# Token pooling and attention merged into one pipeline, with a new output product, on one Trainium2 core

## The reference

```python
def tok(x, w, b):                        # windows of 8 times: 750 -> 94 tokens
    xp = pad(x).reshape(B, F, 94, 8).transpose(0, 2, 3, 1)
    weights = softmax(einsum('bwkf,of->bwko', xp, w) + b, axis=2)
    return sum(xp * weights, axis=2)     # 128 x 94 x 64
def attn(x, Q, K, VO):                   # 8 heads, rank 32
    q = einsum('btd,hrd->bhtr', x, Q); k = einsum('bud,hrd->bhur', x, K)
    a = softmax(einsum('bhtr,bhur->bhtu', q, k) / sqrt(64), axis=-1)
    return einsum('bhtd,hde->bte', einsum('bhtu,bud->bhtd', a, x), VO)
h = tok(x, w, b)
h = h + attn(layernorm(h), Q, K, VO)
h = h + ffn(layernorm(h), ...)           # 4 heads x 4 experts, the same in both kernels
```

## Time and profile before

| | |
|---|---|
| median of 3 runs | 1125.67 us (1123.84 to 1126.86) |
| the profiled execution's own time | 1129.79 us |
| its span | 1128.0 us |
| TensorE busy | 985.3 us (87%) |
| VectorE busy | 931.5 us (83%) |
| ScalarE busy | 674.2 us (60%) |
| GpSimd busy | 676.0 us (60%) |

### The profile page before, as it was taken

One profiled execution on the slowest core, in us unless ns is written; L12 is line 12 of the kernel. 1 busy time (PEld: TensorE's weight loads), 2 busy tenths in 40 slices (PEclk: granted clock), 3 DMA queues, 4 the chain that ended last, 5 costly groups with the idle time before them and its releaser, 6 DMA issues.

```text
span 1128.0 us, 40703 instructions
## 1 busy us (share of the span) xinstructions
PE 985.3 (87%) x16376; PEld 681.6 (60%) x16376; DVE 931.5 (83%) x2061; ACT 674.2 (60%) x1719; POOL 676.0 (60%) x991
## 2 busy tenths in 40 slices
PE   5889878898898988986899999999999999999952
PEld 4667644454454544544677677777777776777741
DVE  3565539999999999982799999999999999999852
ACT  0111137777777777761666767767767667667621
POOL 2000036666656666541048788788888887788786
PEclk9999869999999999996899999999999999999975
DMA  7664300000000000000000001000000000010000
GB/s 256 192 207 125 113 1 2 2 2 2 1 0 0 0 0 0 2 1 6 15 10 15 16 15 23 18 16 20 14 15 19 11 20 18 12 22 19 20 8 14
DMA packets 41576, 35.31 MB, mean 31 GB/s; under 512 B 28160, under 2 KB 31232, under 8 KB 41472
## 3 DMA queue, kind: packets, MB, share of 16 engines
q1 hardware_dynamic: 41376, 33.83, 10.9%
q0 software_dynamic: 96, 0.00, 0.0%
HBM read 24.95 MB, written 3.08 MB: 25 GB/s over the span
## 4 chain that ended last, share of the span: by engine, by line
PE 48%; DVE 25%; POOL 12%; issue 8%; ACT 4%; DMA 1%; DVEq 1%; POOLq 0%; SPq 0%; ACTq 0%
PE psum L733 8%; DVE mx L1569 5%; PE psum L716 4%; PE psum L608 4%; PE psum L623 3%; DVE yc L1611 3%; PE psum L870 3%; PE psum L708 3%; PE psum L881 3%; PE psum L885 3%; PE psum L726 3%; POOL pu L459 3%; DVE xn L1561 2%; PE psum L855 2%; PE psum L889 2%
## 5 line engine op out<-in xcount | busy, mean ns | idle before, releaser
L459 POOL TENSOR_TENSOR pu<-pu,pr 128x752 f32<-128x752 f32 x96 | 138.7, 1444 | 127.7 <-DVE pr L1490 127.7
L524 POOL TENSOR_TENSOR st<-st,neg_half 128x12 f32<-128x12 f32 x64 | 145.8, 2278 | 5.0
L1189 ACT ACTIVATE pu<-psum,mx 128x94 f32<-128x94 f32 x512 | 124.6, 358 | 15.7 <-DVE mx L1481 14.5
L1272 ACT ACTIVATE pT<-psum 96x512 f32<-96x512 f32 (+1 forms) x224 | 126.4, 594 | 6.2 <-PE psum L870 3.3
L1569 DVE TENSOR_REDUCE mx<-psum 128x16 f32<-128x1536 f32 (+2 forms) x96 | 116.6, 1215 | 15.7 <-PE psum L855 11.5
L870 PE MATMUL psum<-ident_w,pu 128*96 128x128 f32 (+1 forms) x896 | 119.9, 275 | 1.9 <-ACT pT L1272 1.5
L1572 DVE TENSOR_TENSOR pu<-psum,mx 128x1536 f32<-128x1536 f32 (+2 forms) x96 | 117.6, 1225 | 3.3
L1266 ACT ACTIVATE pu<-pu 128x1536 f32<-128x1536 f32 (+2 forms) x96 | 101.8, 1060 | 10.0 <-DVE pu L1572 8.2
L733 PEld LDWEIGHTS psum<-vo_w,cT 128*128 128x128 f32 x768 | 90.7, 196 | 24.4 <-issue 13.0
L870 PEld LDWEIGHTS psum<-ident_w,pu 128*96 128x96 f32 (+1 forms) x896 | 100.8, 135 | 6.9 <-ACT pT L1272 4.3
L1422 DVE TENSOR_TENSOR xt<-psum,tok_pT 128x512 f32<-128x512 f32 x96 | 61.4, 684 | 50.5 <-PE psum L608 50.2
(11 more groups left out here) (178 smaller groups left out, 2324.8 us busy)
## 6 DMA issues: line engine op xcount, KB each, us to landing
xs<-in_x SPq DMA_DIRECT2D x64, 375.0 KB, 4.4
vb<-va SPq DMA_DIRECT2D x32, 128.0 KB, 2.3
out_h<-ho SPq DMA_DIRECT2D x128, 16.0 KB, 1.4
out_h<-ho SPq DMA_DIRECT2D x128, 7.5 KB, 1.4
vc<-va SPq DMA_DIRECT2D x96, 16.0 KB, 1.8
gx<-in_L_ffn_gate_w SPq DMA_DIRECT2D x16, 0.2 KB
fc<-in_L_ffn_fc_w SPq DMA_DIRECT2D x12, 1.0 KB
fc<-in_L_ffn_fc_b SPq DMA_DIRECT2D x12, 0.1 KB
```

Source lines behind the costliest of these rows:

```text
L459: pool.tensor_tensor(p, p, bcast(pr[:, j, :, :].rearrange("p a b -> p (a b)"), 2, NTOK), ALU.mult).then_inc(at_normed, 1)
L524: pool.tensor_tensor(st[:, k, 3, :], st[:, k, 2, :], neg_half[:, 0:NJ * NH], ALU.pow).then_inc(rstd, 1)
L1189: ins = act.activation(pu[:, j, par, hp, 0:NTOK], psum[:, (low, high)[par], NTOK * hp:NTOK * hp + NTOK], ACT.Exp, bias=mx[:, j, par, hp:hp ...
L1272: act.activation(pT3[j][:, f - (0, 4, 6)[i], :, :, :].rearrange("p e b t -> p (e b t)"), psum[0:rows, bank, :], ACT.Copy).then_inc(p_copie ...
```

## The change

1. The token and attention stages become one pipeline. Each engine has one function `quad(q)` with four steps, unrolled 48 times in all (no loop). Step `g` works on quad `g + 11` for token scores, on `g + 7` for the token softmax, on `g + 4` to `g + 6` for turning, scaling and pooling, and on `g + 2` down to `g - 3` for attention. Token scores and turned weights share bank 0; all else has banks 1 to 7, each with several users, and the waits for free banks are written out. The order of the calls on each engine was found by a search.
2. `exp_s` asks ScalarE for the sum of each exponential (`accum_out`) into `pl`; VectorE's reduction stays for part 1 only.
3. `give_out` becomes two products: `give_outT` with `vo_w` stationary (128 x 64) and 192 columns of `cT` moving, in two halves of the output columns; `copy_oT` on ScalarE; and a turn back by 64 x 64 products with the identity.
4. `make_g`, `make_w` and `make_w2` move into the pipeline. Groups of `x` are loaded one or two ahead of use as before, but the small loads of the experts' weights stand between groups 2, 3 and 4.

The core of the diff (waits left out where "..." stands):

```diff
                         ins = act.activation(pu[:, j, par, hp, 0:NTOK], psum[:, (low, high)[par], NTOK * hp:NTOK * hp + NTOK], ACT.Exp,
-                                             bias=mx[:, j, par, hp:hp + 1], scale=-1.0)
+                                             bias=mx[:, j, par, hp:hp + 1], scale=-1.0, accum_out=pl[:, j, par, hp:hp + 1])
...
-                dve.tensor_reduce(pl[:, j, :, :], pu[:, j, :, :, 0:NTOK], AX.X, ALU.add).then_inc(done, 1)
-                dve.wait_ge(done, 2 * g + 1)
+                if j in (1,):
+                    dve.tensor_reduce(pl[:, j, :, :], pu[:, j, :, :, 0:NTOK], AX.X, ALU.add).then_inc(done, 1)
+                    dve.wait_ge(done, 2 * g + 1)
                 dve.reciprocal(pr[:, j, :, :], pl[:, j, :, :]).then_inc(done, 1)
...
+            def give_outT(bank):
+                for hp in range(HP):
+                    for half in range(2):
+                        mm = pe.matmul(psum[64 * half:64 * half + 64, bank, 0:NT * 64].rearrange("p (j c) -> p j c", j=NT), vo_w[:, hp, :],
+                                       cT[:, hp, :, 2 * half:2 * half + 2, :].rearrange("p j b t -> p j (b t)"),
+                                       start=(hp == 0), stop=(hp == HP - 1))
+                mm.then_inc(at_outT, 1)
             def give_out(bank):
                 for j in range(NT):
-                    for hp in range(HP):
-                        mm = pe.matmul(psum[:, bank, NFEAT * j:NFEAT * j + NFEAT], cT[:, hp, j, :, :].rearrange("p b t -> p (b t)"), vo_w[:, hp, :],
-                                       start=(hp == 0), stop=(hp == HP - 1))
+                    for half in range(2):
+                        rows = slice(64 * half, 64 * half + 64)
+                        mm = pe.matmul(psum[rows, bank, NFEAT * j:NFEAT * j + NFEAT], oT[rows, j, :, :].rearrange("p b t -> p (b t)"),
+                                       ident[rows, 64 * half:64 * half + 64], start=True, stop=True)
...
+            def copy_oT(bank):
+                act.activation(oT[:, :, :, :].rearrange("p j b t -> p (j b t)"), psum[:, bank, 0:NT * 64], ACT.Copy).then_inc(at_oT, 1)
```

More of the change, by code:

```diff
@@ L341, in _ @@
             for n in range(NH):
-                load(2 + n)
+                if n == 0:
+                    load(2)
                 for e in range(NE):
@@ L368, in _ @@
                 slow(bet[:, 1, HD * i:HD * i + HD], fnorm_b.partition_broadcast(128))
+            for G in range(4, NGROUP):
+                load(G)
             def move_v(p):
@@ L609, in turn @@
                                       xs[:, GP * (G % 2) + 2 * Q + pair, 128 * c:128 * c + 128], ident)
[L610 to L627, removed]
@@ L643, in tok_turn, with make_g @@
                 pe.transpose(tok_P(), tok_e[:, :, :].rearrange("p w k -> p (w k)"), ident[0:TP, 0:TP]).then_inc(tok_turned, 1)
+            def make_g():
+                pe.wait_ge(attn_loaded, 16 * 4)
+                for half in range(2):
+                    for i in range(2):
+                        for par in range(2):
+                            hd = 2 * (2 * i + half) + par
+                            mm = pe.matmul(psum[64 * half:64 * half + 64, 0, 64 * (2 * i + par):64 * (2 * i + par) + 64],
+                                           k_w[:, hd, :], q_w[:, hd, :], start=True, stop=True)
+                mm.then_inc(g_made, 1)
@@ L806, in _ @@
-            for q in range(7, 9):
-                attention(q)
+                        elif exists(g, NQUAD):
+                            pe.wait_ge(at_xT, g + 1)
+                        elif exists(g + 3, NQUAD):
+                            pe.wait_ge(x_scaled, 3 * g + 11)
+                        elif exists(g - 3, NQUAD):
+                            pe.wait_ge(at_cT, 4 * g - 10)
+                        turn(g + 6, 2, 4)
+                    if exists(g + 11, NQUAD):
+                        if exists(g + 7, NQUAD):
+                            pe.wait_ge(tok_ready, ((g + 7) // 4) + 1)
+                        if exists(g + 7, NQUAD):
+                            pe.wait_ge(g_ready, 1)
+                        tok_score(g + 11)
@@ L809, in _ @@
+            for q in range(-3, 9):
+                quad(q)
             pe.wait_ge(causal_set, 10)
@@ new lines, in quad @@
+                    if exists(g, NQUAD):
+                        dve.wait_ge(at_scored, 3 * g + 3)
+                        least(g, 1, 5, 6)
+                        sums(g, 0)
+                    if exists(g + 5, NQUAD):
+                        dve.wait_ge(x_filled, 3 * g + 16)
+                        scale_x(g + 5, 2, 4)
+                    if exists(g, NQUAD):
+                        dve.wait_ge(at_exped, 3 * g + 2)
+                        sums(g, 2)
+                    if exists(g + 7, NQUAD) and (g + 7) % 4 == 0:
+                        dve.wait_ge(tok_scored, g + 11)
+                        soft_tok(g + 7)
@@ L1534, in attention @@
[L1534 to L1545 removed]
+                        dve.wait_ge(at_scored, 3 * g + 4)
@@ L1548, in stats3 @@
+                        least(g + 1, 0, 5, 6)
+            for q in range(-3, 9):
+                quad(q)
+            dve.wait_ge(at_added, NQUAD)
             def stats3(g):
```

676 lines of the change are left out of this document (373 added, 303 removed).

## The result

The changed kernel takes 1054.44 us, against 1124.97 us for the kernel before, run in turn on the same chip: a ratio of 0.937 [0.936, 0.939], 70.5 us saved. Forecast were 1056 us and 69.4 us.

A forecast was written before the change was run, and what follows sets the result against it. VectorE was taken to bound the old attention stage, TensorE the merged pipeline at 12.2 us a quad. Stages summed to 1058.6 against 1128.0 us, 69.4 us saved, so 1056 us from the median 1125.7; range 1028 to 1094.

The forecast's parts named there:

- the part that stays: TensorE's work in the old attention quad without `give_out`: 9.52 - 2.82 = 6.70 us a quad.
- The argument that I gave for it: Old `give_out` pairs follow at 0.12 us, less than their load (2.75/24 = 0.115 us) and a stream.
- The returned sums don't bind: ScalarE: 0.1 us per sum, 9.9 us a quad, below TensorE; rival at 0.3 us each: 1083 us, chance 0.12.
- The rings stand just behind: Merged quad: longest ring of waits found 11.4 us, under TensorE's 11.9 but near, so 2% added: 12.2 us.
- The one that I traced, through `turn_p`: Ring from VectorE's `least` for part 2 over transpose, `project`, `mix` and TensorE's `score` back to `least`: 11.4 us.
- the rival in which it falls: Merged stretch: granted clock falls; at 0.75 the quad takes 15.9 us, 100 us more, 1156 us; chance 0.05.
- first `mix`: End of part one: start, four quads of tokens alone, then 28 us of filling; at 64 us, 8 either way.
- The period: Steady merged quads 12.2 us apart (TensorE's 11.9 us plus 2%); 27 quads, 329.4 us.
- The weight products: `make_w` and `make_w2` moved between quads: 4.5 us once, on TensorE at the full clock.
- The drain: The last two attention quads, taken to drain as in the kernel before: 19.9 us.
- The saving is the token stage laid under attention: The prediction's reason for the 69.4 us saved, paid back by 1.5 us on each of 27 quads.
- VectorE works 10.36 us and bounds the stage: Old attention stage: VectorE's period is 10.74 us a quad with 0.38 us idle, so it was taken as the bound.

The follow-up runs named there:

- e7: The changed kernel with half of `give_outT` left out (two of four head pairs): 1046.44 us, 0.930 of the kernel before.
- e12: The changed kernel in its own order, with the experts' first normalisation done during the drain and the token softmax's bias addition removed: 1040.51 us, 0.923 of the kernel before.
- e3: The changed kernel with parts 2 and 3 both undone, the order of instructions kept: 1121.4 us, 0.995 of the kernel before.
- e1: The changed kernel with part 2 undone, all three `pl` reductions back on VectorE: 1084.74 us, 0.963 of the kernel before.
- e2: The changed kernel with part 3 undone, the old `give_out` back and its addition one quad earlier: 1088.87 us, 0.967 of the kernel before.
- e4: The kernel before with part 2 alone: 1128.49 us, 1.002 of the kernel before.
- e5: The kernel before with part 2, and GpSimd's wait for `mix` before writing `xn` made one quad later: 1130.75 us, 1.007 of the kernel before.
- e6: The kernel before with only GpSimd's wait for `mix` before writing `xn` made one quad later, without part 2: 1125.59 us, 1.0015 of the kernel before.
- e8: The changed kernel with `norm_tok`, the token weights' turn and `copy_tok` moved to other places in every fourth quad: 1064.64 us, 0.944 of the kernel before.
- e10: e8 plus the experts' first normalisation done early, and `pu` part 1 double-buffered, its transpose behind the next quad's `least` for part 1: 1075.39 us, 0.954 of the kernel before.

## Why the prediction was right, step by step

The bound and its size were right: TensorE, at 11.89 us a quad. That the total came within 2 us is in part luck. The span was 1052.4 us where the sum gave 1058.6 us, 6 us less, and its terms were off by up to 5.7 us in both directions. The forecast of the time hides this, as it was counted down from an execution of 1129.79 us, which lay 4.8 us above the median of 1124.97 us.

**TensorE is the bound, at 11.9 us a quad.** Measured 11.89 us. The terms moved against each other: the part that stays took 6.45, not 6.7 us (the two calls of `project` now follow each other, 1.56 instead of 1.70 us); the token work 3.53, not 3.1 us (`tok_score` 1.01, `pool_x` 0.79, three turns 1.69, and a quarter of the 0.17 us of the weights' turn); `give_outT` 1.45, where 1.4 was taken between 0.8 and 1.7; the turn back 0.50, where 0.7 was taken between 0.4 and 1.4. The 0.03 us by which the sum was off are errors of -0.25, +0.43, +0.05 and -0.20 us that cancel. As said, weight loads hide behind running products although both column halves use all 128 rows: a pair takes 1.45/16 = 0.09 us, and one of its loads alone has a record of 0.137 us. The argument that I gave for it does not hold, as 2.75/24 = 0.115 us is the distance from one load to the next and not a load's length; the record of one load of the old product is 0.192 us, at 0.12 us a pair. This is what the Trainium skill ("TensorE: Matmul & The Clock Gate", Part 2) allows with its background weight buffer, and not what its Part 3 would give.

**The returned sums don't bind.** 0.09 us each, 16 x 0.09 = 1.4 us a quad, where 0.1 us was taken between 0 and 0.18. By the Trainium skill ("ScalarE: Activation LUTs", What ACT_TABLE_LOAD costs) one more ACTIVATE of hardly any columns would cost its 186 ns of fixed time less 93 ns of overlap, so 93 ns as an estimate; the page gives no price for the accumulator, but the number fits.

**The rings stand just behind.** 11.4 us was predicted, and 2% laid on top for it. In ordinary quads nothing had to be laid on top. e7 shows a ring of 11.54 us. In the quads without token scores, where TensorE has less to do, a second one of 11.74 us shows, from `least` for part 1 back to itself through the second `project`, `mix` and everything up to the `score` for part 1; TensorE waits 0.65 us for VectorE in it. The one that I traced, through `turn_p`, was not the longest of the three; as no run makes it the bound, its 11.4 us stand untested.

**The clock holds.** 0.99 in the merged stretch; the rival in which it falls did not come.

**The sum by stages,** predicted and measured: first `mix` 64 and 67.5 us; to the 28th `mix` 333.9 and 329.2 us; three quads without tokens 31 and 31.4 us; drain 19.9 and 14.2 us; experts 609.7 and 610.2 us. Errors of +3.5, -4.7, +0.4, -5.7 and +0.5 us make -6 us of span. The terms that were mis-sized:
- *The period.* Ordinary quads 11.89 us, the mean over all but the weight products' excess 11.94 us, against 12.2 us: 7 us less. Every fourth is 12.66 us; the sum had spread the token softmax over four quads, and no term foresaw that it would delay one of them.
- *The weight products.* 6.65 us, against 4.5 us. The products themselves stand on TensorE's timeline for 1.33 + 3.67 = 5.0 us, 0.38 us of it idle. The rest is what follows: from 175.9 to 179.8 us the granted clock is 0.60 and 0.54, near the lower of the two levels, although TensorE had been busy all the time with products of 16 rows, and a `score` takes 1.44 instead of 0.79 us. e12, with another instant of the same work, kept 1.00 there and needed 16.54 - 11.89 = 4.65 us.
- *The drain.* It was taken as before; it fell to 14.2 us, at a granted clock of 0.88 (the window from 428.0 to 442.2 us) instead of 0.74. How much of the 5.7 us is the clock wasn't measured.

**What was wrong is the reason given for the gain.** "The saving is the token stage laid under attention" treats the merge as the gain and the other two parts as small corrections. e3 shows that the merge alone, in this order, gives 0.5%: attention's quad rises from 10.74 to 13.71 us, every fourth to 15.2, a mean of 14.1, where the two stages one after the other pay 10.74 + 3.85 = 14.59 us. The 70 us come from the three together. In the merge alone VectorE's work stands at 12.25 us, TensorE's at 12.78 us and a ring at 13.71 us, and each of the other parts lowers two of the three; with both in, the quad falls to 11.89 us. Undoing part 2, 1.8 us more of VectorE, costs 0.73 us a quad and 30 us in all (e1). Undoing part 3, 0.9 us more of TensorE and the addition moved, costs 1.09 us a quad and 34 us (e2), and both together cost 67 us (e3).

Before the merge the returned sums pay nothing (e4). The step that failed there is my reading of the earlier trace rows, "VectorE works 10.36 us and bounds the stage". The 10.36 us are right, but rings of 10.7 to 10.8 us held the stage (the chains of the kernel before, e4, e5 and e6), and VectorE's idle 0.38 us in each quad agrees with that. The forecast didn't suffer, as its sum for the merged pipeline was made anew from each engine's work. Part 3 alone on the kernel before wasn't tried.

## What to carry to other kernels

Sum the work of each engine and also the rings of waits, and look for how many of them are equal: an engine that is freed pays only as far as the next of them, which can be nothing (e4) or 0.73 of 1.8 us (e1). An engine that is 94% busy but waits in every quad is a hint that a ring bounds, and the chain of work names it. What an edit is worth depends on the state it is put into, so it should be measured by taking it out of the final kernel as well as by putting it alone into the first. Before an instruction is moved, read the timeline at its new place: what is queued behind its wait (e8), and whether the old place lay in a wait that cost nothing (e10).

## What the hardware showed that was not expected

In every fourth quad two small VectorE instructions of the token softmax take longer than in the token stage of before, where the addition `tok_mb` took 0.23 us and the product `tok_e` 0.29 us. The changed kernel's timelines of VectorE and of GpSimd:

```profile
266.19 0.70 DVE L1505 TENSOR_SCALAR tok_mb<-tok_m,tokb 96x16 f32<-96x16 f32 x1
...
269.53 0.54 DVE L1516 TENSOR_TENSOR tok_e<-tok_e,tok_r 96x128 f32<-96x128 f32 x1
```

```profile
265.41 2.85 POOL L466 TENSOR_TENSOR pu<-pu,pr 128x752 f32<-128x752 f32 x2 [4.92 <-DVE pr L1589]
...
269.41 0.51 POOL L457 TENSOR_TENSOR xc<-hj,ln_mv 128x192 f32<-128x192 f32 x1
```

The first of GpSimd's two products ends near 265.41 + 2.85/2 = 266.83 us, and `tok_mb`, begun at 266.19, ends at 266.89 us. `tok_e`, begun at 269.53, ends at 270.07 us, 0.15 us after `xc` (269.92). In e1, where the overlap is longer, the timelines of VectorE and GpSimd give the same picture:

```profile
287.37 1.36 DVE L1505 TENSOR_SCALAR tok_mb<-tok_m,tokb 96x16 f32<-96x16 f32 x1
```

```profile
287.26 1.45 POOL L466 TENSOR_TENSOR pu<-pu,pr 128x752 f32<-128x752 f32 x1 [0.19 <-DVE pr L1588]
```

A 96x16 addition of 0.23 us takes 1.36 us and ends at 288.73, 0.02 us after GpSimd's product (288.71). e8 has moved `tok_e` under such a product (277.19 to 278.64 us), and there it takes 1.27 us:

```profile
277.50 1.27 DVE L1522 TENSOR_TENSOR tok_e<-tok_e,tok_r 96x128 f32<-96x128 f32 x1
```

Each time the small instruction lasts until the GpSimd instruction that it fell under is over. Not every instruction does: beside GpSimd's product in the changed kernel, VectorE's reciprocal at 265.81 takes 0.19 us and the reduction `tok_m` at 265.91 takes 0.24 us, as elsewhere. The Trainium skill ("SBUF — State Buffer", SBUF: two separate sides) describes such an exclusive lock between VectorE and GpSimd, held for a whole instruction, for VectorE's two-port modes and, against a GpSimd instruction that reads SBUF, for its operations with two SBUF inputs. The two instructions here could be one of each; the mode of `tok_mb` is not in the trace, so for it the rule is only compatible.

e12 takes `tok_mb` away, and its `tok_e` product takes 0.29 us again. But it isn't alone there: it begins at 261.30, under an instruction of GpSimd that reads two SBUF operands and by its record lasts until 261.78:

```profile
260.93 0.85 POOL L454 TENSOR_TENSOR ln_rs<-ln_ve,neg_half 128x3 f32<-128x3 f32 x1
```

It is not held up, in any of six quads. So "held for a whole instruction" fits the large products of GpSimd here and not this small power of 128x3; why wasn't looked into. The fourth quads fall from 12.66 to 11.97 us in e12; as it changes the instants as well, it doesn't show how much of that is the lock and how much the shorter work.
